# A fused attention and expert kernel: router scores summed before a 64-column product, expert steps reordered, the last pair normalised by batches with roots as powers

## The reference

```python
x = x + attention(layernorm_c(x))                 # 8 heads, softmax over 8x8 scores per head
t = tokens(x)                                     # (B=8, S=1024, D=64)
u = layernorm(t)
logits = mean(u, axis=1) @ Wr + br                # one row of 8 logits per image
w = softmax(logits); w = softmax(w * min(1, capacity / loads))
top_w, top_i = top_k(w, 2); top_w = softmax(top_w)     # the same 2 experts for all tokens of an image
h = gelu(u @ W1[e] + b1[e]);  y = h @ W2[e] + b2[e]    # F = 128, for both experts e of the image
out = layernorm(sum_e top_w[e] * y_e + u) * gamma + beta
x = t + out
```

## Time and profile before

| | us |
|---|---|
| median of 3 runs (103.19 to 103.4) | 103.39 |
| the profiled execution | 103.3 |
| its span in the trace | 101.5 |
| PE busy | 86.3 (85% of the span) |
| DVE busy | 66.8 (66%) |
| ACT busy | 50.4 (50%) |
| POOL busy | 32.5 (32%) |
| mean granted TensorE clock | 0.967 of full |

### The profile page before, as it was taken

The page is one execution under the profiler, slowest core; times in us unless marked ns, Lnnn a source line. Parts: engine busy times, 40 slices in busy tenths (PEclk is TensorE's granted clock), DMA queues, the critical chain, the costliest instruction groups (busy, mean ns, idle before and its releaser), DMA issues.

```text
span 101.5 us, 2245 instructions
## 1 busy us (share of the span) xinstructions
PE 86.3 (85%) x748; PEld 45.9 (45%) x749; DVE 66.8 (66%) x235; ACT 50.4 (50%) x88; POOL 32.5 (32%) x82
## 2 busy tenths in 40 slices
PE   4997999997999978999869996899999999985200
PEld 1344796896751544699322272323423333341100
DVE  0098998964488998699999527261752726677920
ACT  0000765735666121138578998968877792510000
POOL 7000000008000000044380999472805601960500
PEclk9999999999999999999999999999999999999655
DMA  2999999800000000024200436830000260075075
GB/s 53 287 405 299 287 275 347 217 5 0 0 6 0 0 0 3 6 52 103 52 0 20 96 93 151 201 72 0 6 0 0 65 141 6 0 178 132 0 166 144
DMA packets 6554, 9.82 MB, mean 97 GB/s; under 512 B 1040, under 2 KB 3344, under 8 KB 6544
## 3 DMA queue, kind: packets, MB, share of 16 engines
q1 hardware_dynamic: 4848, 6.77, 25.4%
q10 hardware_dynamic: 1696, 2.92, 10.2%
HBM read 5.49 MB, written 2.10 MB: 75 GB/s over the span
## 4 chain that ended last, share of the span: by engine, by line
PE 69%; DVE 9%; DMA 7%; ACT 4%; issue 4%; ACTq 1%; DVEq 1%
PE pC L1221 14%; DMA cst<-consts_dram 7%; PE pB L917 4%; PE pS L917 4%; PE pA L927 4%; PE pA L1196 3%; PE pB L1196 3%; PE pM L1032 2%; PE pA L990 2%; PE pM L1004 2%; ACT SQ L433 2%; PE pC L1213 2%; PE pS L1066 2%; PE pC L978 2%; PE pS L978 2%
## 5 line engine op out<-in xcount | busy, mean ns | idle before, releaser
L1221 PE MATMUL pC<-H,w2g 128*64 128x512 f32 x64 | 15.8, 602 | 0.0
L484 POOL TENSOR_TENSOR LO<-UF,HI 128x512 f16<-128x512 f32 x8 | 9.2, 1159 | 20.4 <-ACT HI L344 19.5
L610 DVE BATCH_NORM_STATS2 bst<-XT 128x6 f32<-128x128 f32 x32 | 6.5, 282 | 4.9 <-DMA XT<-x_tok_dram 4.9
L1111 PE MATMUL pM<-wz 128*128 128x512 bf16 x25 | 8.0, 491 | 1.3 <-POOL wz L477 1.3
L238 POOL TENSOR_TENSOR XT<-XT,T 128x512 f32<-128x512 f32 x6 | 7.5, 1270 | 4.0 <-DVE XT L879 4.0
L420 ACT ACTIVATE H<-pA,b1s 128x1024 f32<-128x1024 f32 x6 | 6.7, 1111 | 2.5 <-PE pA L1196 2.3
L500 POOL COPY w1g<-w1hl 128x256 f16 x14 | 5.1, 402 | 8.1 <-issue 6.0
L344 ACT CAST HI<-UF 128x512 f16<-128x512 f32 x8 | 4.8, 618 | 5.1 <-DVE UF L718 5.1
L433 ACT ACTIVATE SQ<-pC,c 128x512 f32<-128x512 f32 x8 | 5.4, 686 | 3.8 <-PE pC L1221 3.0
L490 POOL TENSOR_TENSOR w1hl<-SQ,w1hl 128x512 f16<-128x512 f32 x2 | 2.3, 1156 | 15.2 <-DVE A L657 15.2
L855 DVE TENSOR_SCALAR U<-pC,c,wsm 128x512 f32<-128x512 f32 x8 | 6.2, 800 | 1.4 <-PE pC L1221 0.9
(11 more groups left out here) (230 smaller groups left out, 185.8 us busy)
## 6 DMA issues: line engine op xcount, KB each, us to landing
out_dram<-XT SPq DMA_DIRECT2D x14, 128.0 KB, 2.4
XT<-x_tok_dram SPq DMA_DIRECT2D x2, 512.0 KB, 8.9
X<-x_cha_dram SPq DMA_DIRECT2D x8, 128.0 KB, 11.0
X<-x_cha_dram ACTq DMA_DIRECT2D x8, 128.0 KB, 11.1
ST<-HI SPq DMA_DIRECT2D x6, 128.0 KB, 2.4
ST<-LO SPq DMA_DIRECT2D x6, 128.0 KB, 2.4
XT<-x_tok_dram SPq DMA_DIRECT2D x2, 256.0 KB, 4.6
XT<-x_tok_dram ACTq DMA_DIRECT2D x2, 256.0 KB, 4.8
```

What stands on the lines that cost most here:

```text
L484: nc.gpsimd.tensor_tensor(LO[:, p, cols], UF[:, p, cols], HI[:, p, cols], ALU.subtract).then_inc(s["lo"], 1)
L610: return nc.vector.bn_stats(bst[:, p, j, :], XT[:, p, j * P:(j + 1) * P].rearrange("p (b c) -> p c b", b=2))
L1111: mm(pM[:, :], wz[:, 0:P], wz[:, :], start=True, stop=True)
L1221: last = mm(half(y_ps[:, b * HALF:(b + 1) * HALF], h), w2g[:, p % 2, b, k, :], H[:, step % 2, b, h * HALF:(h + 1) * HALF], start=False, st ...
```

## The change

**Router.** `weigh_scores` has one instruction of 256 columns per group where it had two of 128. DVE then sums the four columns of an image (`sum_scores`, two instructions, tile `ssw`), and bias and mean are one product of 64 columns each. The logits and the first softmax live in PSUM: `ps_lg` and `px`, three 64-column pieces of `pB`, in place of `rout`. `centre_w2` is cut in two and stands before the turns of scores 2 and 3, and ACT's copies of its result come first. PE spreads pair 2 ahead of pair 1, and DVE normalises pair 2 first.

**Steps.** POOL does `low(1, 0)` behind the fetches for pair 1 instead of ahead of `wkd`. ACT's `square_z(0)` stands ahead of `gelu` of step 2, `round_hi(3, b)` behind it; DVE's `evac_z(0)` stands ahead of `normal2(3, b)`. `scale_z(p-1, 1)` moves behind `rstd3(p)`. `add_beta` follows steps 3, 4, 5 and 7 in place of 1, 3, 5 and 7. `residual3(0)` is split by batch. In the last pair (`unit`) step 6 does both choices of batch 0, and step 7 those of batch 1.

**Last pair.** Squares, moments, roots and spreads go by batch. The variance stays in float32; POOL raises it to the power -0.5 (`root_last`, 128x8, twice), and PE spreads the root by products of a broadcast column with the identity (`spread_last`, the form of `spread2`), so that bit trick, `split3`, `turn3` and `RR` are gone for this pair. ACT evacuates batch 1 (`evac_z_last`). DVE adds the stream for pair 2, POOL for batch 0 of pair 3. ACT issues half of the output of pairs 2 and 3, SP the other half.

The core of the diff:

```diff
+        def unit(step, i):
+
+            p, n = step // TOP, step % TOP
+            return (p, n, i) if p < NP - 1 else (p, i, n)
...
+        rb3 = [[pS[:, :], pS[:, :]]] * (NP - 2) + [[pS[:, :], pB[:, HALF:N]], [pA[:, 0:HALF], pA[:, HALF:N]]]
+        ps_last = [pM[:, 0:P], pB[:, 0:P]]
+        ps_lg = pM[:, 0:B * E]
+        px = [pB[:, i * B * E:(i + 1) * B * E] for i in range(3)]
...
+            def square_last(b):
+                act.wait_ge(s["mm2"], TOP * NP - 1 + b)
+                cols = slice(b * HALF, (b + 1) * HALF)
+                nc.scalar.activation(SQ[:, 1, cols], y_ps[:, cols], ACT.Square,
+                                     bias=c2[:, B - 2 + b:B - 1 + b]).then_inc(s["sq3"], 1)
...
+            def root_last(b):
+
+                pool.wait_ge(s["mh"], 1)
+                pool.wait_ge(s["red3"], NP + b)
+                cols = slice(b * G2 // 2, (b + 1) * G2 // 2)
+                nc.gpsimd.tensor_tensor(r3[:, NP - 1, cols], v3[:, NP - 1, cols],
+                                        mhalf[:, 0:1].broadcast_to([P, G2 // 2]), ALU.pow).then_inc(s["pow3"], 1)
...
-            add_residual(nc.gpsimd, pool, NP - 2, 0)
-            add_residual(nc.gpsimd, pool, NP - 2, 1)
+            root_last(0)
+            root_last(1)
+            add_residual(nc.gpsimd, pool, NP - 1, 0)
...
+            def sum_scores(g):
+                return nc.vector.reduce_sum(ssw[:, 4 * g * E:4 * (g + 1) * E].rearrange("p (b e) -> p b e", e=E),
+                                            sw[:, 2 * g * P:2 * (g + 1) * P].rearrange("p (b k e) -> p b e k", b=4, e=E),
                                             AX_X)
...
-            link(nc.vector.tensor_scalar(rsm[:, 5, :], rsm[:, 4, :], CAPACITY / N, 1.0, ALU.mult, ALU.min))
+            link(nc.vector.tensor_scalar(rsm[:, 5, :], px[2][:, 0:B], CAPACITY / N, 1.0, ALU.mult, ALU.min))
...
-                mm(ps_lg[g][:, 0:2 * P], ones_m[:, :], sw[:, cols], start=False, stop=True).then_inc(s["lg"], 1)
+                mm(ps_lg, ones_m[:, :], ssw[:, :], start=False, stop=True).then_inc(s["lg"], 1)
...
+            def spread_last(b):
+
+                pe.wait_ge(s["pow3"], NP + b)
+                for k in range(CH // 2):
+                    for h in range(2):
+                        i = b * G2 // 2 + 2 * k + h
+                        last = mm(half(rb3[NP - 1][b][:, k * P:(k + 1) * P], h),
+                                  r3[:, NP - 1, i:i + 1].broadcast_to([P, C]), cf("ident"), start=True, stop=True)
+                last.then_inc(s["rb3"], 1)
```

More of the change, by code:

```diff
@@ L269, in _ @@
                     sp.wait_ge(s_fin[2 * p + b], 1)
-                    for h in range(2 if p < NP - 1 else 1):
+                    for h in range(2 if p < NP - 2 else 1):
                         sp.dma_start(out[b * C:(b + 1) * C, p, h * HALF:(h + 1) * HALF],
@@ L393, in _ @@
                 nc.scalar.copy(w2c[:, h * HALF // 2:(h + 1) * HALF // 2], ps_w2[h]).then_inc(s["w2v"], 1)
+            round_hi(0, 0)
+            act.wait_ge(s["rx1"], 1)
+            nc.scalar.activation(px[0], rout[:, 1, :], ACT.Exp).then_inc(s["rexp1"], 1)
+            round_hi(0, 1)
             nc.scalar.activation(gtab[:, :], w("bout"), ACT.Gelu)
@@ L550, in _ @@
                 experts[0][b] = load_expert(0, 0, b)
-            low(1, 0)
             pool.wait_ge(s["wkd"], 1)
@@ L554, in _ @@
             experts = load_experts(1)
+            low(1, 0)
             low(1, 1)
@@ L753, in _ @@
             weigh_scores(1)
+            for g in range(2):
+                last = sum_scores(g)
+            last.then_inc(s["ssw"], 1)
             normal2(0, 0)
-            read_logits(0).then_inc(s["lr"], 1)
-            link(read_logits(1))
-            dve.wait_ge(s["lr"], 1)
             def be(ap):
@@ L812, in _ @@
             nc.vector.tensor_scalar(wk[:, :, 1], rsm[:, 7, :], 0.5, 0.5, ALU.mult, ALU.add).then_inc(s["wkd"], 1)
-            normal2(2, 1)
             indices(2)
             indices(3).then_inc(s["top"], 1)
-            normal2(1, 1)
+            for b in range(2):
+                normal2(1, b)
             for i in range(4, B):
@@ L1096, in centre_w1, with centre_w2 @@
                        stop=True).then_inc(s["w1p"], 1)
-            def centre_w2():
+            def centre_w2(part):
                 pe.wait_ge(s_w2, 32)
                 pe.wait_ge(s["t"], 2 * NP - 2)
-                for e in range(E // 2):
+                for e in range(part * E // 4, (part + 1) * E // 4):
                     for h in range(2):
@@ L1104, in centre_w2 @@
                                   half(cf("cend"), h)[:, 0:C], start=True, stop=True)
-                last.then_inc(s["w2p"], 1)
+                if part:
+                    last.then_inc(s["w2p"], 1)
             def warm_up(n):
@@ L1158, in _ @@
             scores(2)
+            centre_w2(0)
             turn_scores(2)
             scores(3)
+            centre_w2(1)
             turn_scores(3)
-            bias_logits(0)
-            bias_logits(1)
+            bias_logits()
             spread2(0, 0)
-            logits(0)
-            logits(1)
+            logits()
             spread2(0, 1)
-            centre_w2()
+            for b in range(2):
+                spread2(2, b)
             for b in range(2):
                 spread2(1, b)
-            for b in range(2):
-                spread2(2, b)
             pe.wait_ge(s["w1h"], 2)
@@ L1209, in residual3 @@
                     pe.wait_ge(s["sq3"], 2 * p)
-                pe.wait_ge(s_st[p + 1 if p else 1], 64)
-                for b in range(2):
+                for b in batches:
+                    if p == 0:
+                        pe.wait_ge(s_uf[4 + b], 1)
+                    pe.wait_ge(s_st[p + 1 if p else b], 64)
                     for h in range(2):
```

280 lines of the change are left out of this document (154 added, 126 removed).

## The result

The changed kernel takes 97.41 us (median of four) against 103.4 us for the kernel before on the same chip: ratio 0.942, 95% interval 0.9395 to 0.9442. The forecast was 96.7 in a range of 95.6 to 99.8. In the profiled executions the span falls from 101.5 to 95.7 us.

The account below looks back on a forecast made before the run. PE, with 69% of the chain, was taken as the bound nearly everywhere until about 86.6 us. Gains of 2.3 (to the moments of pair 1), 3.4 (last pair) and 0.9 (output) make 6.6: 103.3 to 96.7 us, range 95.6 to 99.8.

Parts of the forecast that it names:

- Router: Start of the kernel: logits at 42.0, PE done with spreads at 46.65, 2.0 us earlier, and `top` at 46.0.
- Last pair: From the moments of pair 2 to the last add: last add at 93.55 instead of 96.95, gain 3.4 us.
- The step on the PSUM reads: Router: L777 and L767 on DVE now read PSUM, so their waits beside POOL's work were taken as gone.
- What survives of it: Start of the experts: SP's back-to-back issues let only 0.4 to 0.7 of the router's 2.0 us survive at `first_up(1)`.
- the forecast 2.3: Gain from the front up to the moments of pair 1: 2.3 us, between 0 and 2.9.
- The road that the forecast took: POOL's chain to step 4: `wkd` at 49.9, copies, four `low`, start at 64.6 against 67.14, gaining 2.5 us.
- the price of the root: Last pair: POOL's power for one root takes 0.7 us, the middle between 0.218 and 1.26 us.
- that rival's own formula: Rival, roots dear or late (15%): above 1.5 us each, the last add ends at 88.0 + 2P + 2.4.
- my 91.1: Last pair: when PE has done 2 idle products, a spread of 16 at 1.0 and 3 idle products.
- the signs of being wrong: Root above 1.5 us, PE waiting over 0.5 for `LO` or `w1g`, clock 0.5 before last spread, transfers still 4.5 after last add.
- Output: Last add to end: 4.55 us before; pair 2 added 3 us earlier and ACT issuing its share gain 0.9 us.
- Clock: Last pair's spreads: full clock expected; rival of a falling clock (6%), 1.0 us more for each of two spreads, 97.7 to 98.7.

Follow-up runs that it names:

- px_sbuf: The changed kernel with only the router tiles `px` back in SBUF, the logits staying in PSUM; 98.26 us, ratio 0.9487.
- dve_order: The changed kernel with `scale_z(p - 1, 1)` ahead of `rstd3(p)` on DVE again; 99.64 us, ratio 0.9665.
- root_mult: The changed kernel with POOL's power in the last pair's roots replaced by a product, leaving the root out; 97.43 us, ratio 0.9411.
- mult_no_awake: The changed kernel with that power replaced by a product and without the idle products around the last two spreads; 96.96 us, ratio 0.9374.
- out_sp: The changed kernel with all of pair 2's output transfers issued by SP, none by ACT; 98.2 us, ratio 0.948.
- no_awake: The changed kernel without the idle products around the last two spreads, power kept; 97.83 us, ratio 0.9457.

## Why the prediction was right, step by step

**Router, too early by 0.9 us.** `top` was to come at 46.0 and came at 46.86. DVE began to weigh at 40.28, not at 40.07, and the two sums took 1.13 us, not 0.84 ("each at the 0.42 us of a 256-column reduction"), so that the logits' product started at 42.38, where the logits were to be there at 42.0. And "`normal2(0, 1)` ends at 43.0 + 0.65" failed: PE's spread for it runs behind the logits product, DVE waited 0.55 us for it (row at 43.89), and it ended at 44.58. The step on the PSUM reads held, and px_sbuf shows it. "If the PSUM reads saved nothing, 46.6, still hidden by PE" was wrong: 0.57 us at `top` cost 0.85.

**What survives of it.** The first expert product was forecast at 47.2 and started at 48.15, waiting 0.81 us for `ST`. Of the 2.0 us, 0.4 to 0.7 were to survive at `first_up(1)`, and nothing did: it starts at 50.17, before at 50.12. The step that failed is "the last at 47.35 instead of 47.71": SP's last issue came at 47.97. That SP's transfers cap this point was right. Rows of PE in the kernel before, behind its 50.12:

```profile
51.61 0.61 PE L1196 MATMUL pA<-HI,w1g 64*128 64x512 f16 x4 [0.46 <-ACT H L420]
52.91 0.62 PE L1213 MATMUL pC<-ST,cstb 128*64 128x512 f16 x4 [0.48 <-issue]
53.34 1.05 PE L1221 MATMUL pC<-H,w2g 128*64 128x512 f32 x4
```

The gain comes on PE itself, behind that point. Before, PE waited 0.46 us for the first `gelu`; now the first product is 1.0 us earlier, so is its `gelu`, and the next product follows at 51.14 without a wait. Before, PE also waited 0.48 us ahead of `residual3`, where the profile names nobody (DVE's last read of pair 2's spread, in the same `pC`, ends at 52.82); now DVE normalises pair 2 first and has read `pC` by 50.31. The second half of `residual3(0)` now stands behind the first down. So that down starts at 52.13, 1.21 us earlier. (These causes are read from the rows; none was taken away by itself.) PE keeps 1.1 us of that and comes to the moments of pair 0 at 61.46, where it came at 62.57 before and then waited 1.21. That makes 2.32 us, of which 0.27 are given back before the moments of pair 1, as said at dve_order: 2.05 of the forecast 2.3. The road that the forecast took, from `wkd` by POOL's copies and `low` to step 4, ran beside it and ended almost level: `wkd` at 50.82 (forecast 49.9), 3.2 us to the copies instead of 3.6, and step 4 at 64.96 for a forecast 64.6 by POOL; PE alone, forecast for 64.3, would have started it at 64.82. The sum came out near because both roads are equally long, which is luck in part.

**Last pair, 2.6 of 3.4.** The last down ends at 85.38 (84.9 forecast), the last add at 92.29 (91.3). Of the 0.5 us at the last down 0.25 come from the front, and most of the rest is a slip in adding: 82.8 with four downs at 0.93, 0.35, 0.15 and 0.35 makes 87.4, not 87.2. The step that failed is the price of the root: "a power is more work per element than either, so I take the middle, 0.7", with 1.26 as the upper end. An add of 64 times the elements was no upper bound for an operation that costs 0.16 us and more an element of a partition, where that add costs 1.26 / 512 = 0.0025. 1.65 and 1.96 us are above the 1.5 from which I had two roots in a row set the end; with 1.8 in that rival's own formula, 88.0 + 3.6 + 2.4 = 94.0 instead of 93.55, 0.45 later, or 97.15 us. Its mechanism is there in the trace, but barely: the second root ends at 89.61 and the last spread starts at 89.67, while PE's idle products have ended at 88.71 + 0.82 = 89.53. So it costs no more than the 0.2 us by which root_mult's tail is shorter, because PE's own work ends nearly as late: the transposition 0.5 us later than forecast (87.3 against 86.8), and the idle products at 0.59 and 0.82 against the 1.05 that my 91.1 leaves for both. My working had these terms and took them too small; the two errors lie side by side and don't add. What comes behind is also short by 0.3: from the start of the last spread to the end of the last add it is 92.29 - 89.67 = 2.62 us, not 93.55 - 91.2 = 2.35. That a root 2.5 times as dear as forecast cost so little is luck, not foresight.

**The signs.** Of the signs of being wrong one came, a root above 1.5 us. PE did not wait over 0.5 us for `LO` or `w1g`: at step 2 it was nothing, at step 4 0.14.

**A step that was right without being named.** The sum began at the moments of pair 2 with "columns to 82.8" and four downs with a spread among them. That needs pair 2's root in time, which hangs on the exchange of `rstd3` and `scale_z(p - 1, 1)` on DVE. I never spoke of it, and dve_order shows 1.7 us on it: this too was luck.

**DVE beside POOL.** I had the second root start between 89.3 and 90.6, as DVE's adds might hold it up. The second root costs 0.3 us more than the first, as a power (1.96 to 1.65) and as a product (0.52 to 0.20). The Trainium skill (SBUF — State Buffer, "Who interferes with whom") says that a DVE instruction with two SBUF inputs contends with a POOL instruction that reads SBUF, and calls what they share an exclusive lock. I made of it a wait for both of DVE's adds, which that section does not say. In mult_no_awake the adds take 87.28 to 88.58 and the product is done at 88.03: no wait for both; a wait for the rest of the first fits it, and so does the rule taken instruction by instruction.

**Output, 1.14 of 0.9.** The size is about right, the reason only half: not ACT's share of the issues, as out_sp shows; that pair 2's early adds are what empties SP's queue is inferred from the order.

**Clock.** At full until the last spread, as forecast (1.00 in the window from 90 to 92 us); the trace of no_awake shows that without the idle products it can fall, as long as the roots are dear.

## What to carry to other kernels

Idle time of the weight loader is not idle time of PE: loads run ahead of the matmuls, so read PE's own row, and set it beside the same place in the kernel before. An "old order" put back into a changed kernel also moves what is new in it; here `gc` came onto the path that way and made 0.76 us of the answer. A bound on an unknown operation must come from the same kind of work: size alone (64 times the elements of another operation) bounds nothing, and a scratch run of the operation at two sizes settles it. Where one suspect is taken away and nothing moves, look for what stands in parallel to it in the waiting engine's own program, and take away both: the power and the idle products were each worth nothing and together 1.08 us of tail. When work is moved ahead on one engine, check each producer's queue for what stands in front of the operand that is now wanted earlier; here the exchange of two lines on DVE was worth 1.7 us, more than the 1.1 of roots and idle products.
